# Decoder layer, cross-attention: row maxima split on VectorE, transposed as eight columns, and moved by one transfer per pair of heads

## What is computed

```python
q = (x @ Wq).reshape(B, N, HEADS, hd)          # 16 heads of 32
k = (context @ Wk).reshape(B, M, HEADS, hd)    # M = 750 keys
v = (context @ Wv).reshape(B, M, HEADS, hd)
scores = jnp.where(context_mask, q k^T * scale, max_neg)
attn = jax.nn.softmax(scores, axis=-1)         # subtracts each row's maximum
out = (attn v) @ Wo
```

## Time and profile before

| | us |
|---|---|
| median of 3 runs | 3769.72 (3767.74 to 3772.16) |
| the profiled execution, its own time | 3775.88 |
| span of its trace | 3774.1 |
| busy in the span: TensorE, VectorE, ScalarE, GpSimd | 3639.7 (96%), 2361.0 (63%), 1731.9 (46%), 1305.9 (35%) |
| granted TensorE clock, mean | 0.982 of full speed |
| cross-attention | about 1080 to 2430 of the span |

### The profile page before, as it was taken

How to read it: one execution, slowest core, us unless ns; L and a number is a source line. 1 busy time by engine, 2 the same in 40 slices (tenths; PEclk the granted TensorE clock), 3 DMA queues, 4 the chain that set the end, 5 groups by cost and what they waited for, 6 DMA issues and landing times. The chain is left out here.

```text
span 3774.1 us, 84215 instructions
## 1 busy us (share of the span) xinstructions
PE 3639.7 (96%) x28244; PEld 3139.7 (83%) x28244; DVE 2361.0 (63%) x5543; ACT 1731.9 (46%) x4278; POOL 1305.9 (35%) x1388
## 2 busy tenths in 40 slices
PE   8999999999979999999999999849999999999999
PEld 7888888888868888888888888638998899989998
DVE  6888888888846666666666666576433434434343
ACT  4555555555435555555555555413333333333332
POOL 2333333333325656666556566510101101011010
PEclk9999999999989999999999999869999999999999
DMA  4222222222243434444434343223324334234232
GB/s 127 60 54 63 54 63 53 64 53 64 72 122 94 112 106 104 108 116 107 121 96 113 104 108 97 71 68 94 121 82 122 107 98 123 82 118 123 85 108 69
DMA packets 315057, 349.72 MB, mean 93 GB/s; under 512 B 45308, under 2 KB 232036, under 8 KB 314884
## 3 DMA queue, kind: packets, MB, share of 16 engines
q1 hardware_dynamic: 305796, 318.26, 30.7%
q0 software_dynamic: 9088, 29.17, 2.4%
HBM read 183.23 MB, written 38.91 MB: 59 GB/s over the span
## 5 line engine op out<-in xcount | busy, mean ns | idle before, releaser
L1627 DVE TENSOR_REDUCE x_mx<-x_psS 112x1 f32<-112x752 f32 x512 | 479.7, 937 | 382.2 <-PE x_psS L1180 378.6
L2423 DVE TENSOR_TENSOR hid<-e_psU,act_g 128x280 f32<-128x280 f32 x256 | 115.1, 450 | 622.6 <-PE e_psU L34 585.8
L1462 ACT ACTIVATE x_pt<-x_psE 125x448 f32<-125x448 f32 x768 | 389.6, 542 | 227.6 <-PE x_psE L1192 217.7
L1051 POOL TENSOR_TENSOR part<-x_pt 125x448 f32<-125x448 f32 x255 | 292.4, 1147 | 506.0 <-ACT x_pt L1462 497.1
L2049 POOL DMA_INDIRECT out<-ex_y,sidx x40 | 39.8, 995 | 1020.4 <-DVE ex_y L2457 1010.2
L635 POOL TENSOR_TENSOR qks<-qks,cos 128x448 f32<-128x448 f32 x128 | 148.1, 1157 | 657.0 <-DMA qks<-qk 657.0
L1180 PE MATMUL x_psS<-k_st,q_st 97*112 97x376 f32 x1024 | 287.9, 362 | 24.1 <-DMA k_st<-mk 16.3
L32 PE MATMUL e_psG<-ex_hi,g_hi 128*128 128x280 f32 x1024 | 304.2, 297 | 6.7 <-ACT act_g L2208 4.5
L32 PE MATMUL pj<-xT_hi,win_hi 128*128 128x224 f32 x1024 | 302.2, 295 | 4.0 <-PEq L185 3.9
L2208 ACT ACTIVATE act_g<-e_psG 128x280 f32<-128x280 f32 x256 | 103.7, 405 | 426.4 <-PE e_psG L34 412.1
L1053 POOL TENSOR_TENSOR part<-part,x_pt 125x448 f32<-125x448 f32 x255 | 292.3, 1146 | 20.0
(11 more groups left out here) (305 smaller groups left out, 10890.3 us busy)
## 6 DMA issues: line engine op xcount, KB each, us to landing
k_st<-kT SPq DMA_DIRECT2D x768, 93.8 KB, 2.2
raw_g<-in_L_ffn_wg SPq DMA_DIRECT2D x128, 256.0 KB
raw_u<-in_L_ffn_wu SPq DMA_DIRECT2D x128, 256.0 KB
raw_d<-in_L_ffn_wd SPq DMA_DIRECT2D x128, 256.0 KB
qks<-qk SPq DMA_DIRECT2D x512, 56.0 KB, 2.0
q_st<-qT SPq DMA_DIRECT2D x384, 56.0 KB, 2.0
ctxt<-in_ctx SPq DMA_DIRECT2D x16, 1125.0 KB
xt<-in_x SPq DMA_DIRECT2D x16, 448.0 KB, 3.7
```

Source lines behind the costliest of these rows:

```text
L1051: pool.tensor_tensor(part[:], pt[j][:, 0, :], pt[j][:, 1, :], ALU.add).then_inc(parted, 1)
L1462: act.activation(pt[j][:, i, :], psE[(j + i) % 2][0:KR, 0:2 * T], ACT.Exp, scale=XD ** -0.5).then_inc(exp_done, 1)
L1627: dve.tensor_reduce(mx[:, j, h:h + 1], psS[0:HT, :, 0:376], AX.XY, ALU.max).then_inc(s_taken, 1)
L2423: dve.tensor_tensor(h[ring][:, halves[s]], psU[:, 0:CH], act_g[i][:, halves[s]], ALU.mult).then_inc(S["mul"], 1)
```

## The change

Each maximum pair is now split on VectorE before the transposition: `split_max` writes minus the maximum, rounded, into columns 0 to 3 of `m_parts`, and the remainder into columns 4 to 7 (two heads by two halves). TensorE transposes these eight columns at once into 8 partitions x 112. ScalarE's `out_max` copies that to `m_row` (8 x 112), and SyncE moves `m_row` into rows 97 and 98 of `q_st` by one transfer (`place_max`). TensorE waits for that transfer (`m_placed`). `m_row` has one buffer: `out_max` waits for the transfer before. `high_max` and `low_max` are gone.

```diff
+                    def place_max(u, g, i):
+                        hold(sp, gate, pj_free[u.bank], u.after)
+                        head = 4 * g + 2 * i
+                        sp.dma_start(q_st[97:99, head:head + 2, :].bitcast(F32), m_row[:].bitcast(F32)).then_inc(m_placed, 16)
...
                     def body(b, first, last, more):
                         t = 4 * b
+                        near, far = range(2), range(2, 4)
+                        if not first:
+                            place_max(unit_of(b, "M1_0"), 3, 1)
                         if not last:
                             load_ctx(b + 1)
-                        place_k(t + 1, b, 1, [unit_of(b, "K10"), unit_of(b, "K11")])
-                        place_q(b, 1, [unit_of(b, "Q2"), unit_of(b, "Q3")])
+                        k_units = [unit_of(b, "K10"), unit_of(b, "K11")]
+                        place_k(t + 1, b, 1, k_units, near)
+                        place_max(unit_of(b, "M0_0"), 0, 0)
+                        place_k(t + 1, b, 1, k_units, far)
+                        q_units = [unit_of(b, "Q2"), unit_of(b, "Q3")]
+                        place_q(b, 1, q_units, near)
+                        place_max(unit_of(b, "M1_1"), 0, 1)
+                        place_q(b, 1, q_units, far)
...
                     def turn_max(u, t, i):
-                        pe.wait_ge(s_taken, 8 * t + 4 * i + 4)
+                        pe.wait_ge(m_split, 4 * t + 2 * i + 2)
                         o = bank(u)
-                        for n in range(4):
-                            m = pe.transpose(o[:, n * HT:(n + 1) * HT], mx[:, 2 * i + n // 2, n % 2:n % 2 + 1].to_broadcast((HT, P)),
-                                             ident[0:HT, 0:HT])
-                        m.then_inc(pj_full, 1)
+                        pe.transpose(o[0:8, 0:HT], m_parts[:, i, :].bitcast(F32), ident[0:HT, 0:HT]).then_inc(pj_full, 1)
...
                                 scores(n, g, j, 0)
+                                if j == 3:
+                                    turn_max(U(f"M0_{g}"), n, 0)
                                 if prev:
-                                    if j == 0:
-                                        done(U(f"M0_{gp}") if g else unit_of(b - 1, "M0_3"))
-                                    elif j == 2:
-                                        done(U(f"M1_{g}"))
+                                    if j in (0, 2):
+                                        pe.wait_ge(m_placed, max_placed(n - 1, j // 2))
                                     shifted(n - 1, gp, j, (0, 1))
...
-                    def high_max(u, g, i):
+                    def out_max(u, t, i):
+                        if i or not below(t, 1):
+                            act.wait_ge(m_placed, max_placed(t, i) - 16)
                         o = full(u)
-                        act.activation(q_st[96:99, 4 * g + 2 * i:4 * g + 2 * i + 2, :],
-                                       o[96:99, 0:2 * T].rearrange("p (j t) -> p j t", j=2), ACT.Identity,
-                                       bias=ident[96:99, 96:97], scale=ident[96:99, 98:99]).then_inc(m_high, 1)
+                        act.activation(m_row[:], o[0:8, 0:HT], ACT.Copy).then_inc(pj_free[u.bank], 1)
...
-                    def low_max(u, n, g, i):
-                        dve.wait_ge(m_high, n)
-                        rows = q_st[96:99, 4 * g + 2 * i:4 * g + 2 * i + 2, :]
-                        dve.scalar_tensor_tensor(rows, pj[u.bank][96:99, 0:2 * T].rearrange("p (j t) -> p j t", j=2),
-                                                 less[96:99, 0:1], rows.bitcast(F32), ALU.mult, ALU.add).then_inc(pj_free[u.bank], 1)
+                    def split_max(t, i):
+                        raw = mx[:, 2 * i:2 * i + 2, :]
+                        hi, lo = (m_parts[:, i, k:k + 4].rearrange("p (j h) -> p j h", j=2) for k in (0, 4))
+                        dve.wait_ge(s_taken, 8 * t + 4 * i + 4)
+                        dve.tensor_scalar(hi, raw, -1.0, None, ALU.mult).then_inc(m_split, 1)
+                        dve.wait_ge(m_split, 4 * t + 2 * i + 1)
+                        dve.scalar_tensor_tensor(lo, raw, -1.0, hi.bitcast(F32), ALU.mult, ALU.subtract).then_inc(m_split, 1)
```

More of the change, by code:

```diff
@@ L914, in k_mult, with max_placed @@
                 return 16 * (4 if g < 2 else 3)
+            def max_placed(t, i):
+                return 32 * t + 16 * i + 16
+            fills = [ones[:]] + [k[96:99, :].bitcast(F32) for k in k_st]
             def placed(b, g):
@@ L958, in store_rows, with place_k @@
                         sp.dma_start(at(rv, b, "o p h d -> (o p) h d"), xr[:]).then_inc(xr_stored, 16)
[L960 to L968, removed]
+                    def place_max(u, g, i):
+                        hold(sp, gate, pj_free[u.bank], u.after)
+                        head = 4 * g + 2 * i
+                        sp.dma_start(q_st[97:99, head:head + 2, :].bitcast(F32), m_row[:].bitcast(F32)).then_inc(m_placed, 16)
+                    def place_k(t, b, g, units, heads=range(4)):
+                        if 0 in heads:
+                            for u in units:
+                                hold(sp, gate, pj_free[u.bank], u.after)
+                            if g == 0:
+                                hold(sp, gate, mask_step, 3 * b + 3)
+                            if below(t, 1):
+                                sp.wait_ge(filled, len(fills))
+                        for j in heads:
                             if not below(t, 2):
@@ L979, in place_k, with place_q @@
                                 sp.dma_start(slot[96:97, :].bitcast(F32), mk[96:97, :]).then_inc(k_placed[j], 16)
[L981 to L987, removed]
+                    def place_q(b, half, units, heads=range(4)):
+                        if 0 in heads:
+                            for u in units:
+                                hold(sp, gate, pj_free[u.bank], u.after)
+                            if not below(b, 1):
+                                hold(sp, gate, st_full, 48 * b - 24 + 24 * half)
+                        for j in heads:
                             rows = slice(32 * j, 32 * j + 32)
@@ L1015, in body @@
                         if not last:
-                            place_q(b + 1, 0, [unit_of(b, "Q0"), unit_of(b, "Q1")])
-                        if not last:
-                            place_k(t + 4, b + 1, 0, [unit_of(b, "K00"), unit_of(b, "K01")])
+                            q_units = [unit_of(b, "Q0"), unit_of(b, "Q1")]
+                            place_q(b + 1, 0, q_units, near)
+                            place_max(unit_of(b, "M1_3"), 2, 1)
+                            place_q(b + 1, 0, q_units, far)
+                            k_units = [unit_of(b, "K00"), unit_of(b, "K01")]
+                            place_k(t + 4, b + 1, 0, k_units, near)
+                            place_max(unit_of(b, "M0_3"), 3, 0)
+                            place_k(t + 4, b + 1, 0, k_units, far)
+                        else:
+                            place_max(unit_of(b, "M1_3"), 2, 1)
+                            place_max(unit_of(b, "M0_3"), 3, 0)
                     body(0, True, False, True)
@@ L1037, in _ @@
                 def _(pool):
[L1039 to L1042, removed]
+                    for n, f in enumerate(fills):
+                        pool.memset(f, 1.0).then_inc(filled, 1)
                         pool.wait_ge(filled, n + 1)
-                    pool.nop().then_inc(zeroed, 1)
                     def sum_blocks(t, g, heads=range(4)):
@@ L1246, in first_gap @@
                         def first_gap(g, j):
-                            n, nxt, ng = t + g, not (last and g == 3), (g + 1) % 4
+                            nxt, ng = not (last and g == 3), (g + 1) % 4
                             if j < 2 and nxt:
@@ L1357, in _ @@
                     turn_rows(last("N1_14"), B - 2, 1)
-                    done(last("M1_4"))
+                    pe.wait_ge(m_placed, max_placed(n - 1, 1))
                     shifted(n - 1, 3, 2, range(3))
@@ L1513, in second_gap @@
                         def second_gap(g, j):
-                            gp, prev = (g + 3) % 4, not (first and g == 0)
                             if j == 0:
@@ L1522, in second_gap @@
                                     out_v(U("V00"), 0, 0)
-                                if prev:
-                                    high_max(U(f"M1_{g}"), gp, 1)
+                                if not (first and g == 0):
+                                    out_max(U(f"M1_{g}"), t + g - 1, 1)
                             elif j == 1:
@@ L1576, in _ @@
                     n = 4 * B
-                    exps(n - 1, 0, range(3))
-                    high_max(unit_of(B - 1, "M1_4"), 3, 1)
-                    for j in range(1, 4):
+                    out_max(unit_of(B - 1, "M1_4"), n - 1, 1)
+                    for j in range(4):
                         exps(n - 1, j, range(3))
```

(3 more changed lines are left out.)

39 lines of the change are left out of this document (22 added, 17 removed).

## The result

| | before | after |
|---|---|---|
| median (lowest to highest) | 3771.2 us (3767.7 to 3777.2, 6 runs) | 3839.8 us (3835.2 to 3844.0, 6 runs) |
| ratio, with its 95% interval | 1 | 1.0181 [1.0169, 1.0193] |
| span of the profiled execution | 3774.1 us | 3837.8 us (+63.7) |

What follows compares the result with a forecast made beforehand. TensorE's queue was taken to bound the kernel, busy 82.5 of 83.3 us a batch. Terms 42 + 16 - 5 - 9.5 + 2 = +45.5 us on the median 3769.7 gave 3815 us, range 3780 to 3848.

Steps and rivals of the forecast that it cites:

- start of group 1 and M0_0: Group 1's scores and first `shifted` wait for late k and M0_0 transfers: 3.0 us in 14 batches, +42 us.
- the clock: TensorE's granted clock falls after the longer wait in two of three batches, 1.7 us each: +16 us (0 to 24).
- waits and fall of before: Today's 3.5 us of mask-row waits and 1.7 us clock loss drop out of the sum: -5 us.
- M1's shorter transposition: TensorE does one transposition instead of four for M1, saving 0.6 us a batch: -9.5 us over 16 batches.
- VectorE's order, group 2: Operations added on VectorE were taken to cost nothing, as it idles about a third of a batch or more: 0.
- ends: Partly uncovered maxima transfers in the last batch, and M0_0 behind the context in the first: +2 us (0 to 4).
- The start of the context load times the start of group 1: On SyncE, head 0 of group 1 lands 14.4 to 14.9 us after the context load starts, now 2.3 us later.
- Rival 3: Faster: the context load's start doesn't matter to k's landing, only M1's gain and ends stay: about 3758 us, chance 0.10.
- M0_0's transfer lands with head 1's last: In group 1 M0_0's transfer, queued behind both heads of k, lands at 1699.4 to 1699.9; TensorE needs it at 1696.73.
- "This costs and gives nothing" on VectorE and ScalarE: Both idle about a third of a batch or more, so their changed operations cost nothing; uncovered, `low_k` is 0.7 us late.
- The other seven transfers cost nothing beyond M1_1: Each adds 0.64 to 0.84 us on SyncE; k and q behind them are needed half a group later.
- M1_1 hides only because TensorE is late; alone it costs 1.0: M1_1's transfer behind half of q lands at 1706.7, needed at 1705.73 + 3.0; without that lateness it costs 1.0 us.

Runs made afterwards that it cites:

- e6_ctx_and_split: Changed kernel with the context load in two transfers of 112 and 13 partitions and `split_max` behind residual and `low_k` in head step 1: 3753.1 us, 0.9940 of before.
- e3_before_ctx_held: Kernel before, with one added wait: SyncE holds the next context load until the bank of M1_0 is free; no maxima transfer: 3854.3 us, 1.0213 of before.
- e2_ctx_112_13: Changed kernel with the context load in two transfers, of 112 and 13 partitions, instead of one of 125: 3784.1 us, 1.0029 of before.
- e1_split_late: Changed kernel with `split_max` behind residual and `low_k` in VectorE's head step 1 instead of ahead of them: 3822.2 us, 1.0126 of before.
- e5_ctx_first: Changed kernel with the next context load, still one transfer, ahead of M1_0's transfer instead of behind it: 3931.3 us, 1.0416 of before.
- e8_all_ctx_first: Changed kernel with context split 112/13, `split_max` late, M1_1's transfer ahead of all q, and context and mask loads ahead of M1_0's transfer: 3824.6 us, 1.0141 of before.
- e9_all_three: Changed kernel with context load split 112/13, `split_max` behind residual and `low_k`, and M1_1's transfer ahead of all q transfers: 3749.6 us, 0.9933 of before.
- e4_before_ctx_112_13: Kernel before, with the context load in two transfers of 112 and 13 partitions: 3763.8 us, 0.9973 of before.
- e7_before_ctx_held_less: Kernel before, with the next context load held on SyncE only until TensorE has ended M1_0's transpositions: 3803.0 us, 1.0078 of before.

## Why the prediction came out as it did

The direction and the mechanism were right. The time lay inside the range of 3780 to 3848 but 8 us above the likeliest case's own 3800 to 3832; the sum was +45.5 where the spans differ by 63.7. Term by term, over 14 batches:

| term | predicted | measured |
|---|---|---|
| start of group 1 and M0_0 | 42 | 48: 40.5 in group 0, 7.4 in group 1 |
| the clock | 16 | 22: 12 falls of 1.0 to 2.4 |
| waits and fall of before | -5 | -5 |
| M1's shorter transposition | -9.5 | -10 outside group 0 (14 x 0.71) |
| VectorE's order, group 2 | 0 | 10.5: 14 x 0.75 |
| ends | 2 | -3.2 |

The 40.5 are the +37.0 of group 0 and the 3.5 us that it waited before; a fall is what group 1 takes above the 23.0 us of the batch whose clock held, and the 7.4 are what is left in group 1 with M1's gain and the fall of before set against it. These add up to 62; 1 to 2 us are not placed.

**The start of the context load times the start of group 1**: right. It started 2.65 us later from the batch's first scores (predicted 2.3), and its 14.4 to 14.9 us to the landing of head 0 were 14.6 in the batch shown, 14.8 in the mean. The copy took 0.24 us (0.3) and the issue 0.74 (0.64 to 0.84). M1_0's copy is not the whole account of that start: SyncE's queue was itself 1.7 us late there, and reached M1_0's transfer about when the copy was done. In `e6_ctx_and_split`, where the queue is 0.2 us less late, M1_0's transfer goes out 0.2 us after the end of the copy and the load starts 2.4 us later than before. So the copy and the transfer account for up to 2.4 of the 2.65 us; the queue's lateness runs beside them, and overlooking it cost the forecast little here. `e3_before_ctx_held` shows that the delay alone makes such a loss, `e2_ctx_112_13` that without the narrow load there is none in group 0. Rival 3, in which it doesn't matter, is out.

**M0_0's transfer lands with head 1's last**: right in size. TensorE had it 5.2 us after its issue, at 1725.48, head 1's L992 at 1725.14. The part of the maxima that the prediction called certain is there, but as about 0.5 us a batch: most of the wait is k's mask row.

**The clock**: the mechanism was right, the size off. Two batches in three were taken at 1.7 us; it was 12 of 14 at 1.8 in the mean. The one earlier fall gave a fair price; the share of the batches was a guess, and came out too low.

**"This costs and gives nothing" on VectorE and ScalarE**: the step that failed. It rested on the idle share of VectorE over a batch, and on the mask's issue as the cover of `low_k`. The first says nothing of what stands behind the new operations in the queue: in group 2 that is the residual, which sets a PSUM bank free, and TensorE waited 0.75 us for it in 13 or 14 batches. `e1_split_late` takes this wait away. The second was right only while the mask's issue was 3.8 us long: once it is 0.37, `split_max` makes `low_k` 1.35 us late (0.7 was named), and with it k and M1_1's transfer. The same operations ahead of `low_k` in group 3 make group 0's k 0.75 us late, ahead of the context load. Each operation was bounded at 0.37 us by the nearest row; one took 0.64 and one 1.10 in the places shown, 0.42 and 0.36 in the mean.

**The other seven transfers cost nothing beyond M1_1**: failed as well. "What waits behind a maxima transfer in SyncE's queue (far k, far q) is needed half a group later" is true of k itself, but the context load stands behind it, and M0_3's transfer delays that load by 0.9 us. In the changed kernel the wait for M1_0's copy covers most of it; in `e5_ctx_first` and `e8_all_ctx_first` it is paid in full.

**M1_1 hides only because TensorE is late; alone it costs 1.0**: right in kind. With group 0 on time it cost about 1.4.

**M0 gives nothing**: right; head step 3, where it stands, is within 0.02 us of before in all four groups of `e9_all_three` against `e4_before_ctx_112_13`. **M1 0.6 a batch**: 0.18, 0.19, 0.29 and 0.23 in the four groups, 0.89 together, of which the first is swallowed by the wait.

## What to carry to other kernels

A transfer put into a queue ahead of a long one delays the long one, and everything that needs the engines behind it; one put behind it waits for it. Look at how many engines the long one uses before choosing an order: here splitting 125 partitions into 112 and 13 took away 41 us of waits, where each of the two orders tried lost. With the load split the order still counts: 3749.6 us with the maxima's transfer first, 3824.6 behind the load. Look, too, at what was added further ahead in the same queue and in the engine that this queue waits for: here that alone made the load 1.7 us late. Price an operation added to an engine with idle time by what stands right behind it in its queue, and who waits for that, not by the idle share. And a wait that a larger wait hides must be priced for the day when the larger one is mended.

## What the runs showed of the hardware that was not expected

- The clock is not set by the length of the last wait alone. It fell after 1.86 us in the kernel before and in 12 of 14 batches after some 2.9 us, held after 2.70 and 2.95, and held after all 14 waits of up to 2.3 us in one profiled execution of `e7_before_ctx_held_less`. After the 14 waits of 3.4 to 4.5 us in `e3_before_ctx_held` it fell every time. What else decides stays open.
- A transfer of a few KB behind a 1125 KB load and a mask load took 8.9 us, from its issue to TensorE's next matmul, where the big load had five engines and 6.2 where it had all (`e5_ctx_first`, `e8_all_ctx_first`), against 1.9 us with nothing long just ahead (`e2_ctx_112_13`).
- The issue of the mask's load behind the load on five engines held SyncE 3.8 us, behind the same load on all engines 0.37. No run shows why.
- The same VectorE operation on 112 x 4 took from 0.17 to 0.64 us, its companion from 0.16 to 1.10, in the places shown. The cause is not known.
